# Two experts' rows per token added up in memory by the indirect transfers, instead of on VectorE in the last stage

## The chip, the cores and the metric

The kernel runs on one core of one Trainium2 chip. The metric is the device time of one execution in microseconds (us): 1415.3 us, the median of three runs of the kernel before (1413.99 to 1415.97).

## The reference

Two layers over x of 4 batches x 1024 tokens x 128 channels, float32. Each layer normalises x, computes an attention s and a gate g from it, and gives x + s * g. In the second layer, the gate is the silu of a mixture of experts:

```python
gates = softmax(xf @ Wg.T)                      # xf: T = 4096 tokens x 128
topw, topi = top_k(gates, 2)                    # two different experts for each token
C = round(2 * T * 1.05 / 8)                     # 1075 rows for each of the 8 experts
# each expert takes at most C (token, choice) entries, first choices first
h = gelu(rows @ W1[e] + b1[e]); y = h @ W2[e] + b2[e]
out[t] = sum over k of topw[t, k] * y[topi[t, k], position]     # 0 for an entry over the capacity
x = x + s * silu(out)
```

## The kernel before, in words

One program of seven stages, each a block in which every engine has its own list of instructions, ordered by semaphores. A stage begins when all engines have ended the one before. The two stages `inverse_and_routing` and `layer1_attention` also dispatch: for each of the two choices k, 32 indirect transfers (`dispatch`, L1259 to L1262) write 128 tokens' rows each into the memory table `x_disp`, at the row of the expert and position that the token was given. A row has 130 elements: the 128 channels, the number of the entry (k * 4096 + token, plus 1; 0 in a row that nobody fills) and its weight. `mark_entries` (L1252) sets the last two columns ahead of each k. `x_disp` and the result table `y_tok` are zeroed in pieces of about 1 MB by SyncE during the first layer's attention (`zero`, L804), one piece in each of the first `PIECES` = 18 turns of its loop (14 pieces for `x_disp`, 4 for `y_tok`).

`experts` (from L1701) treats the eight experts one after the other, as j = 0 to 3 and buffer c = 0 or 1. SyncE loads an expert's 1075 rows (9 tiles of 128, the last of 51) and weights. TensorE transposes the rows (L1843), multiplies by W1 (L1855), and, after the gelu on ScalarE (L1835), by W2 in three groups of tiles (L1865). VectorE copies the transposed rows (L1779), works out where each row's result goes (L1784 to L1789: `wt`, `free`, `dest`), adds the bias (L1800) and multiplies by the weight (L1807). Before L1784 VectorE waits until the transfers out of this buffer for the expert two earlier have landed (L1782). SyncE's load of the next rows into a buffer waits for `dest`. GpSimd then sends the rows by nine indirect transfers per expert (L1765), each as soon as its group has been multiplied. A row goes to row `k * 4096 + token` of `y_tok`, so no two experts write the same row; results of unfilled rows go to spare rows behind. The last expert has groups of 3, 3 and 3 tiles, and its matmuls are interleaved. GpSimd waits for all landings before the stage ends (L1768).

`combine` (from L1911) works in 8 parts of 4 token tiles (128 x 512 elements). SyncE issues two loads per part, one per choice (L1955, 16 in all, 256 KB each), VectorE adds the two (L1935), ScalarE takes the silu (L1946), VectorE multiplies by the attention (L1928) and adds to x (L1930), and SyncE stores the part (L1959). SyncE's stores stand behind all its loads. VectorE does the next part's sum before it finishes a part.

Of the kernel before, what the change touches and what calls it, by code (L numbers as in the profile page):

```python
# [12 lines left out]
P = 128  # L13
# [13 lines left out]
NPAIR = B * PAIRS  # L27
E, TOPK = 8, 2
CAP = int(round(TOPK * B * T * 1.05 / E))
ENTRIES = TOPK * B * T  # L30
XT = -(-CAP // P)
LASTROWS = CAP - (XT - 1) * P
HID = 512
# [35 lines left out]
def make(nc, ctx, ins):  # L69
    g = Program()  # L70
    g.nc = nc
    (g.x_in, g.ln_scale, g.ln_bias, g.w_qkv, g.w_proj, g.b_proj, g.W_r, g.W_k, g.W_v, g.mu_r, g.mu_k,
     g.W_attn, g.W_proj, g.Wg, g.W1, g.b1, g.W2, g.b2, g.out) = ins
    g.sb = lambda name, shape, dt=F32: ctx.enter_context(nc.sbuf_tensor(name, shape, dt))
    sems = {}

    def sem(name):
        if name not in sems:
            sems[name] = nc.alloc_semaphore(name=name)
        return sems[name]  # L80

    cleared = []

    def clear(eng, prefix):

        for name in [n for n in sems if n.startswith(prefix)]:
            eng.sem_clear(sems[name])
            cleared.append(sems.pop(name))

    def release():  # L90

        while cleared:
            nc.release_semaphore(cleared.pop())

    g.sem, g.clear, g.release = sem, clear, release
    g.dram = lambda name, shape, dt=F32: nc.dram_tensor(name, shape, dt, kind="Internal").ap()
    g.ps = ctx.enter_context(nc.psum_tensor("psum", [P, 8 * BANK], F32))
    g.bank = lambda k, n=1: g.ps[:, k * BANK:(k + n) * BANK]


    g.X = g.sb("x_res", [P, NT, D])
    g.XNW = g.sb("x_norm", [P, NT, ROW])
    g.XN = g.XNW[:, :, 0:D]
    g.G = g.sb("gate_or_attn", [P, NT, D])

    g.ident = g.sb("ident", [P, P])
    g.wqkv0 = g.sb("wqkv0", [P, 3, P])
    g.wproj0 = g.sb("wproj0", [P, P])
    g.wr2 = [g.sb(f"wr{i}", [P, P]) for i in range(2)]
    g.wk2 = [g.sb(f"wk{i}", [P, P]) for i in range(2)]  # L110
    g.wvT = g.sb("wvT", [P, P])
    g.wqkv1 = g.sb("wqkv1", [P, 3 * P])
    g.wproj1 = g.sb("wproj1", [P, P])
    g.wgT = g.sb("wgT", [P, E])
    g.b1T = g.sb("b1T", [P, E * HC])
    g.cols = g.sb("cols", [P, 8])
    g.bproj = g.sb("bproj", [P, P])
    g.eps_pow = g.sb("eps_pow", [P, TB])
    g.mask4 = g.sb("mask4", [P, 4])
    g.headmask = g.sb("headmask", [P, H])  # L120


    g.q_ops = g.dram("q_ops", [QUADS, HQ, NPART, HD, T], BF16)
    g.k_ops = g.dram("k_ops", [QUADS, HQ, 2 * NPART - 1, HD, T], BF16)
    g.v_ops = g.dram("v_ops", [QUADS, P, HQ, TB * 2 * HD])
    g.av_out = g.dram("av_out", [QUADS, HQ, 2 * HD, T])
    g.x_disp = g.dram("x_disp", [E * CAP + ENTRIES, ROW])
    g.y_tok = g.dram("y_tok", [ENTRIES + 2 * XT * P, D])
    g.recs = g.dram("recs", [B, H, T])
    g.q1_keep = g.dram("q1_keep", [B, P, T])  # L130
    return g
# [43 lines left out]
E_RING = 12  # L175
DISP_ROW = CAP * ROW // 5
DISP_PIECES = -(-DISP_ROW // 2048)
PIECES = DISP_PIECES + ENTRIES * D // P // 2048
LOADS0 = 16 * (4 * NPART + 1)
STORED = (48, 48, 32)  # L180

# [383 lines left out]
def layer0_attention(g):  # L565
# [31 lines left out]
    with nc.Block() as block:  # L597
# [183 lines left out]
        @block.sync  # L781
        def _(sp):
            def store_maxima(d):


                for i in range(NPART):
                    if i == 0:
                        sp.wait_ge(sem("b_max_done"), seq.index((d, None)) + 1)
                    else:
                        sp.wait_ge(sem(("b_second", "b_third")[i - 1]), d + 1)  # L790
                    dst = q[d // 2 % SLOTS][ROWS + i:ROWS + i + 1, 2 * (d % 2):2 * (d % 2) + 2, :]
                    sp.dma_start(dst.rearrange("r h (t x) -> r (h t) x", x=P), neg[:, i, :])\
                      .then_inc(sem("b_m_loaded"), 16)

            def store_values(d):
                sp.wait_ge(sem("b_acc"), d + 1)
                for i in range(4):
                    dst = g.av_out[d // 2, 2 * (d % 2) + i // 2, :, i % 2 * BANK:(i % 2 + 1) * BANK]
                    sp.dma_start(dst, acc[32 * i:32 * i + 2 * HD, d % 2, :]).then_inc(sem(f"b_stored{d % 2}"), 16)

            disp = g.x_disp[0:E * CAP, :].rearrange("(q r) d -> q (r d)", q=E * 5)
            kept = g.y_tok[0:ENTRIES, :].rearrange("(q r) d -> q (r d)", q=P)

            def zero(piece):  # L804
                i = 2048 * piece
                if piece < DISP_PIECES:
                    n = min(2048, DISP_ROW - i)
                    sp.dma_start(disp[:, i:i + n], zeros[0:E * 5, 0:n]).then_inc(sem("disp_zeroed"), 16)
                else:
                    i -= 2048 * DISP_PIECES  # L810
                    sp.dma_start(kept[:, i:i + 2048], zeros[:, :]).then_inc(sem("disp_zeroed"), 16)

            for c in range(1, SLOTS):
                load_quad(g, sp, c, c)
            store_maxima(0)
            sp.wait_ge(sem("b_zeros"), 1)
            for d in range(DUOS):
                if d + 1 < DUOS:
                    store_maxima(d + 1)
                store_values(d)  # L820
                if d < PIECES:
                    zero(d)
                if d % 2 and d // 2 + SLOTS < QUADS:

                    sp.wait_ge(sem("b_av"), TB * (d + 1))
                    wait_for_parts(g, sp, (d // 2 + SLOTS) // 4)
                    load_quad(g, sp, d // 2 + SLOTS, d // 2 % SLOTS)
            for s in range(2):
                sp.wait_ge(sem(f"b_stored{s}"), 16 * 4 * QUADS)
            sp.wait_ge(sem("disp_zeroed"), 16 * PIECES)  # L830

# [419 lines left out]

def mark_entries(g, link, k):  # L1252

    link(g.nc.gpsimd.tensor_scalar(g.XNW[:, :, D:D + 1], g.iof[:, E + k * NT:E + (k + 1) * NT].unsqueeze(2),
                                   float(1 - E * CAP), None, ALU.add))
    link(g.nc.gpsimd.tensor_copy(g.XNW[:, :, D + 1:D + 2], g.CW[:, k, :].unsqueeze(2)))


# [451 lines left out]
def experts(g):  # L1710
# [31 lines left out]
    with nc.Block() as block:  # L1742
# [11 lines left out]
        @block.gpsimd  # L1754
        def _(pool):
            nc.gpsimd.tensor_scalar(unused[:, :, :], g.iof[:, E:E + 2 * XT].rearrange("p (c t) -> p c t", c=2),
                                    float(ENTRIES + 1 - E * CAP), None, ALU.add).then_inc(sem("e_unused"), 1)
            for j in range(E // 2):
                for c in range(2):
                    pool.wait_ge(sem("e_dest"), ex(j, 1, c, 1))  # L1760
                    for i, (lo, hi) in enumerate(groups(j, c)):
                        pool.wait_ge(sem("e_y"), ex(j, 3, c, i + 1))
                        for t in range(lo, hi):
                            r = rows(t)
                            pool.indirect_dma_start(g.y_tok[:, :], bass.IndirectOffsetOnAxis(dest[c][0:r, t:t + 1], 0),  # L1765
                                                    y[c][0:r, t, :], None).then_inc(sem(f"e_sent{c}"), 16)
            for c in range(2):
                pool.wait_ge(sem(f"e_sent{c}"), SENT * (E // 2))  # L1768

# [141 lines left out]
def combine(g):  # L1911

    nc, sem = g.nc, g.sem
    with ExitStack() as mem:
        sb = lambda name, shape, dt=F32: mem.enter_context(nc.sbuf_tensor(name, shape, dt))
        yk = sb("g_y", [P, TOPK, NT, D])
        f = sb("g_f", [P, NT, D])
        sg = sb("g_sg", [P, NT, D])
        spare = sb("g_spare", [P, 1])
    part = lambda i: slice(i * NT // PARTS, (i + 1) * NT // PARTS)  # L1920
    with nc.Block() as block:

        @block.vector
        def _(dve):
# [5 lines left out]
                nc.vector.tensor_tensor(g.X[:, s, :], g.X[:, s, :], sg[:, s, :], ALU.add).then_inc(sem("g_x"), 1)  # L1930

            for i in range(PARTS):
                s = part(i)
                dve.wait_ge(sem(f"g_loaded{i}"), 16 * TOPK)
                nc.vector.tensor_tensor(f[:, s, :], yk[:, 0, s, :], yk[:, 1, s, :], ALU.add).then_inc(sem("g_f"), 1)  # L1935
                if i >= 1:
                    finish(i - 1)
            finish(PARTS - 1)

        @block.scalar  # L1940
        def _(act):
            act.activation(spare[:, :], g.eps_pow[:, 0:1], ACT.Silu).then_inc(sem("g_spare"), 1)
            for i in range(PARTS):
                s = part(i)
                act.wait_ge(sem("g_f"), i + 1)
                act.activation(sg[:, s, :], f[:, s, :], ACT.Silu).then_inc(sem("g_sg"), 1)  # L1946

        @block.sync
        def _(sp):
            src = g.y_tok[0:ENTRIES, :].rearrange("(k n p) d -> p k n d", p=P, k=TOPK)  # L1950
            dst = g.out.rearrange("b (n p) d -> p (b n) d", p=P)
            for i in range(PARTS):
                s = part(i)
                for k in range(TOPK):
                    sp.dma_start(yk[:, k, s, :], src[:, k, s, :]).then_inc(sem(f"g_loaded{i}"), 16)  # L1955
            for i in range(PARTS):
                s = part(i)
                sp.wait_ge(sem("g_x"), i + 1)
# [43 lines left out]
```

## Time and profile before

| | |
|---|---|
| Median of three runs | 1415.3 us |
| The profiled execution's own time | 1400.87 us |
| Its span in the trace | 1399.1 us |
| Busy in the span: PE, DVE, ACT, POOL | 90%, 72%, 62%, 17% |
| Expert stage, from its first matmul to the start of the last stage | 1225.7 to 1375.3 us |
| Last stage | 1375.3 to 1399.1 us |

Times in the trace are counted from the start of its span. PE is TensorE, PEld its weight loads, DVE VectorE, ACT ScalarE, POOL GpSimd, SPq SyncE's queue of transfer issues. A POOL DMA_INDIRECT row shows the time that GpSimd needs to issue the transfer, and not the movement of the data. "Idle before" is the time in which an engine had nothing running ahead of an instruction, with the instruction that ended it.

### The profile page before, as it was taken

To read this page: it belongs to the slowest core of one execution; us is meant where nothing else is said; L and a number is where in the kernel's file an instruction comes from. 1 tells how busy PE (TensorE), PEld (TensorE's weight loads), DVE (VectorE), ACT (ScalarE), POOL (GpSimd) and SP (SyncE) were. 2 spreads that over 40 slices of the span, in tenths; PEclk is the share of its full clock that TensorE was granted. 3 is DMA by queue.
4 is the path that set the end of the run, shared out by engine and by line. 5 is a ranking of instruction groups with operands and counts; after the bars stand their busy time and mean duration, and the time that the engine had idled before them with its cause. 6 is when DMAs were issued, how large, how long until landed. Compare 5 with 4: busy or idle time off the path is not lost. (4 is left out here: it accounts for less than half of the span.)

```text
span 1399.1 us, 26250 instructions
## 1 busy us (share of the span) xinstructions
PE 1265.2 (90%) x10433; PEld 595.5 (43%) x10433; DVE 1009.8 (72%) x1309; ACT 864.0 (62%) x1459; POOL 236.2 (17%) x306
## 2 busy tenths in 40 slices
PE   6967999999999999999999988898899899999990
PEld 4631222222222222222222235555699666678870
DVE  6877888898998988899899637665756388623324
ACT  3533878788887787888888855555132466543331
POOL 4200110000000000000000011100644222125560
PEclk9976999999999999999999989999999699999995
DMA  4763133331334323322120021100001111123316
GB/s 145 214 189 67 32 67 84 71 71 47 67 86 98 108 78 72 67 62 48 27 64 10 6 55 33 46 16 15 18 28 34 59 35 43 47 65 99 100 57 186
DMA packets 75206, 94.98 MB, mean 68 GB/s; under 512 B 13236, under 2 KB 44684, under 8 KB 74052
## 3 DMA queue, kind: packets, MB, share of 16 engines
q1 hardware_dynamic: 69996, 83.19, 23.6%
q0 software_dynamic: 5088, 10.12, 2.3%
q8 instruction: 82, 1.34, 0.4%
q14 instruction: 40, 0.33, 0.1%
HBM read 54.30 MB, written 38.56 MB: 66 GB/s over the span
## 5 line engine op out<-in xcount | busy, mean ns | idle before, releaser
L664 ACT ACTIVATE b_exp_ring<-psum 128x512 f32<-128x512 f32 x1024 | 555.5, 599 | 158.2 <-PE psum L719 155.0
L606 DVE TENSOR_REDUCE b_mx<-psum 128x2 f32<-128x1024 f32 x507 | 595.8, 1219 | 75.9 <-PE psum L551 74.8
L719 PE MATMUL psum<-b_q,b_k 75*128 75x512 bf16 x1024 | 311.9, 387 | 10.7 <-DMA b_q<-b_neg 9.1
L695 PE MATMUL psum<-b_exp_ring,b_v 128*32 128x512 f32 x2048 | 274.5, 608 | 0.9 <-ACT b_exp_ring L664 0.7
L719 PEld LDWEIGHTS psum<-b_q,b_k 75*128 75x128 bf16 x1024 | 79.2, 97 | 328.4 <-ACT b_exp_ring L664 223.6
L550 PE MATMUL psum<-b_k,b_q 64*128 64x512 bf16 x512 | 169.0, 395 | 25.4 <-DVE b_mx L606 10.5
L551 PE MATMUL psum<-b_ko,b_qo 64*128 64x512 bf16 x512 | 169.0, 395 | 0.0
L734 POOL CAST b_neg<-b_neg_rest 16x128 bf16<-16x128 f32 x32 | 8.9, 280 | 661.4 <-DVE b_neg_rest L617 661.4
L1835 ACT ACTIVATE e_hT<-psum,e_b 128x358 f32<-128x358 f32 (+3 forms) x96 | 53.7, 560 | 75.6 <-PE psum L1855 72.3
L550 PEld LDWEIGHTS psum<-b_k,b_q 64*128 64x128 bf16 x512 | 44.1, 93 | 127.5 <-DVE b_mx L606 41.8
L695 PEld LDWEIGHTS psum<-b_exp_ring,b_v 128*32 128x32 f32 x2048 | 41.2, 108 | 108.2 <-issue 106.4
L1261 POOL DMA_INDIRECT x_disp<-x_norm,row_sent x64 | 62.5, 976 | 122.1 <-PE psum L1633 81.4
L1765 POOL DMA_INDIRECT y_tok<-e_y,e_dest x72 | 70.8, 984 | 70.7 <-DVE e_y L1807 51.5
L1865 PE MATMUL psum<-e_w,e_hT 128*128 128x128 f32 (+1 forms) x576 | 67.4, 277 | 0.0
L1569 DVE TENSOR_REDUCE f_max<-psum 128x16 f32<-128x1024 f32 x32 | 39.2, 1225 | 37.3 <-PE psum L1633 36.5
L1865 PEld LDWEIGHTS psum<-e_w,e_hT 128*128 128x128 f32 (+1 forms) x576 | 64.6, 184 | 1.8
L1613 ACT ACTIVATE f_le<-f_lx 128x1024 f32<-128x1024 f32 x32 | 33.8, 1057 | 47.3 <-DVE f_lx L1575 47.3
L1855 PE MATMUL psum<-e_xT,e_w 128*128 128x358 f32 (+3 forms) x192 | 60.2, 468 | 0.9 <-DVE e_xT L1779 0.9
L991 DVE TENSOR_REDUCE c_nm<-psum 128x1 f32<-128x1024 f32 x32 | 37.7, 1220 | 31.7 <-PE psum L1148 31.6
L1411 ACT ACTIVATE i_aq<-psum 128x1024 f32<-128x1024 f32 x20 | 20.5, 1024 | 58.7 <-PE psum L1434 58.7
L1095 ACT ACTIVATE c_en<-psum,c_nm 128x1024 f32<-128x1024 f32 x32 | 35.7, 1117 | 32.1 <-DVE c_nm L991 32.1
L1434 PE MATMUL psum<-i_x,i_aq 64*64 64x64 f32 x1536 | 46.2, 218 | 1.4 <-DVE i_x L1380 1.4
(281 smaller groups left out, 1487.4 us busy)
## 6 DMA issues: line engine op xcount, KB each, us to landing
b_q<-q_ops SPq DMA_DIRECT2D x48, 192.0 KB
b_k<-k_ops SPq DMA_DIRECT2D x48, 192.0 KB
k_ops<-a_k SPq DMA_DIRECT2D x20, 256.0 KB, 3.2
x_disp<-b_zeros SPq DMA_DIRECT2D x13, 320.0 KB
e_x<-x_disp SPq DMA_DIRECT2D x8, 520.0 KB
v_ops<-a_vs SPq DMA_DIRECT2D x4, 1024.0 KB, 5.1
b_v<-v_ops SPq DMA_DIRECT2D x16, 256.0 KB
av_out<-b_acc SPq DMA_DIRECT2D x128, 32.0 KB, 1.7
```

Of the source, the lines that this page charges most:

```text
L550: g.nc.tensor.matmul(g.bank(2 * (n % 2)), q[0:MROWS, 2 * p, t], k[0:MROWS, 2 * p, keys], start=True, stop=True)
L551: return g.nc.tensor.matmul(g.bank(2 * (n % 2) + 1), qo[MROWS:P, p, t], ko[MROWS:P, p, keys], start=True, stop=True)
L606: nc.vector.reduce_max(mx[:, d % 2, :, i // 2, i % 2], pair, AX.X).then_inc(sem("b_max_done"), 1)
L664: act.activation(ex[:, n % E_RING, :], g.bank(5 + n % 3), ACT.Exp, scale=ATT_SCALE)\
L695: last = nc.tensor.matmul(AV[32 * i:32 * i + 32, :], v[s][:, at_v:at_v + 32], ex[:, (4 * group + i) % E_RING, :], start=(kb == 0), stop=(k ...
L719: nc.tensor.matmul(g.bank(5 + n % 3), k[s][0:XROWS, h, kb * P:(kb + 1) * P], q[s][0:XROWS, h, half * BANK:(half + 1) * BANK], start=True, ...
L1261: pool.indirect_dma_start(g.x_disp[:, :], bass.IndirectOffsetOnAxis(g.rows_out[:, n:n + 1], 0), g.XNW[:, n % NT, :], None).then_inc(g.sem( ...
L1434: last = nc.tensor.matmul(out[half, i, :], lhs(n * GR + i, half), rhs(n * GR + i, half), start=True, stop=True)
L1765: pool.indirect_dma_start(g.y_tok[:, :], bass.IndirectOffsetOnAxis(dest[c][0:r, t:t + 1], 0), y[c][0:r, t, :], None).then_inc(sem(f"e_sent ...
L1835: act.activation(hT[c][:, i, lo:hi], g.ps[:, (3 + n % 3) * BANK:(3 + n % 3) * BANK + hi - lo], ACT.Gelu, bias=b1[c][:, i:i + 1]).then_inc( ...
L1855: nc.tensor.matmul(g.ps[:, (3 + n % 3) * BANK:(3 + n % 3) * BANK + hi - lo], w1[c][:, i * P:(i + 1) * P], xT[:, lo:hi], start=True, stop=T ...
L1865: last = nc.tensor.matmul(g.ps[0:r, col:col + D], hT[c][:, i, t * P:t * P + r], w2[c][:, i, :], start=(i == 0), stop=(i == HC - 1))
```

## The change

`y_tok` with a row per entry becomes `y_sum` with a row per token. The number in a dispatched row is that of the token, whichever choice it is, so `mark_entries` writes that column for k = 0 only. The indirect transfers of the experts add their rows to the table (`compute_op=ALU.add`). As a token's two experts now write the same row, GpSimd waits, ahead of each expert's transfers, until those of the expert before have landed. Only 2 pieces of the table are zeroed, where 4 were. The last stage loads one row per token, takes its silu and does the two operations that are left on VectorE.

```diff
-PIECES = DISP_PIECES + ENTRIES * D // P // 2048
+PIECES = DISP_PIECES + TOKENS * D // P // 2048
...
-    link(g.nc.gpsimd.tensor_scalar(g.XNW[:, :, D:D + 1], g.iof[:, E + k * NT:E + (k + 1) * NT].unsqueeze(2),
-                                   float(1 - E * CAP), None, ALU.add))
+    if k == 0:
+        link(g.nc.gpsimd.tensor_scalar(g.XNW[:, :, D:D + 1], g.iof[:, E:E + NT].unsqueeze(2),
+                                       float(1 - E * CAP), None, ALU.add))
...
                 for c in range(2):
                     pool.wait_ge(sem("e_dest"), ex(j, 1, c, 1))
+                    if c or j:
+                        pool.wait_ge(sem(f"e_sent{1 - c}"), SENT * (j + c))
                     for i, (lo, hi) in enumerate(groups(j, c)):
                         pool.wait_ge(sem("e_y"), ex(j, 3, c, i + 1))
                         for t in range(lo, hi):
                             r = rows(t)
-                            pool.indirect_dma_start(g.y_tok[:, :], bass.IndirectOffsetOnAxis(dest[c][0:r, t:t + 1], 0),
-                                                    y[c][0:r, t, :], None).then_inc(sem(f"e_sent{c}"), 16)
+                            pool.indirect_dma_start(g.y_sum[:, :], bass.IndirectOffsetOnAxis(dest[c][0:r, t:t + 1], 0),
+                                                    y[c][0:r, t, :], None, compute_op=ALU.add).then_inc(sem(f"e_sent{c}"), 16)
...
             for i in range(PARTS):
-                s = part(i)
-                dve.wait_ge(sem(f"g_loaded{i}"), 16 * TOPK)
-                nc.vector.tensor_tensor(f[:, s, :], yk[:, 0, s, :], yk[:, 1, s, :], ALU.add).then_inc(sem("g_f"), 1)
-                if i >= 1:
-                    finish(i - 1)
-            finish(PARTS - 1)
+                finish(i)
...
-                act.wait_ge(sem("g_f"), i + 1)
-                act.activation(sg[:, s, :], f[:, s, :], ACT.Silu).then_inc(sem("g_sg"), 1)
+                act.wait_ge(sem(f"g_loaded{i}"), 16)
+                act.activation(sg[:, s, :], yk[:, s, :], ACT.Silu).then_inc(sem("g_sg"), 1)
...
-                for k in range(TOPK):
-                    sp.dma_start(yk[:, k, s, :], src[:, k, s, :]).then_inc(sem(f"g_loaded{i}"), 16)
+                sp.dma_start(yk[:, s, :], src[:, s, :]).then_inc(sem(f"g_loaded{i}"), 16)
```

## Rows read from the trace of the kernel before

**Rows 1.** Windows: us, busy (count) of PE, PEld, DVE, ACT, POOL; clock, DMA share, GB/s.

```profile
1242.49:1259.33 16.84, 16.84 (x108) 13.58 (x107) 5.14 (x13) 6.71 (x12) 8.92 (x10) 1.00 0.24 68
...
1343.54:1375.30 31.76, 17.85 (x116) 14.51 (x114) 5.32 (x12) 6.72 (x12) 17.69 (x18) 0.81 0.12 35
1375.30:1399.10 23.80, 0.00 (x0) 0.00 (x0) 15.34 (x24) 6.52 (x10) 0.00 (x0) 0.50 0.98 265
```

**Rows 2.** Timeline of the last stage (start, us, operation [idle before]), then the chain's start.

```profile
1379.56 0.69 DVE L1935 TENSOR_TENSOR g_f<-g_y 128x512 f32<-128x512 f32 x1 [16.87 <-DMA g_y<-y_tok]
1380.29 0.63 ACT L1946 ACTIVATE g_sg<-g_f 128x512 f32<-128x512 f32 x1 [3.40 <-DVE g_f L1935]
...
1382.11 0.69 DVE L1928 TENSOR_TENSOR g_sg<-g_sg,gate_or_attn 128x512 f32<-128x512 f32 x1
...
1382.83 0.69 DVE L1930 TENSOR_TENSOR x_res<-x_res,g_sg 128x512 f32<-128x512 f32 x1
1383.44 0.69 DVE L1935 TENSOR_TENSOR g_f<-g_y 128x512 f32<-128x512 f32 x1
...
1395.74 0.69 DVE L1930 TENSOR_TENSOR x_res<-x_res,g_sg 128x512 f32<-128x512 f32 x1
...
1375.38 0.38 SPq L1955
...
1375.81 0.50 SPq L1955
```

**Rows 3.** DMA view of the last stage, 1375 to 1399.1 us, in 40 slices.

```profile
GB/s 0 0 54 249 332 275 185 252 320 334 293 298 292 296 292 291 287 292 291 289 292 290 287 293 290 289 292 321 349 343 348 343 347 345 235 303 133 246 190 0
```

**Rows 4.** Timeline around the third expert's first transfer; the other boundaries look the same.

```profile
1259.32 1.00 POOL L1765 DMA_INDIRECT y_tok<-e_y,e_dest  x1 [5.48 <-DVE e_y L1807]
...
1269.53 1.08 POOL L1765 DMA_INDIRECT y_tok<-e_y,e_dest  x1 [0.30 <-issue]
...
1272.25 0.17 DVE L1784 COPY e_wt<-e_x 128x9 f32<-128x9 f32 x1 [1.35 <-DMA y_tok<-e_y,e_dest]
...
1274.34 0.69 DVE L1800 TENSOR_TENSOR e_y<-psum,e_b 128x512 f32<-128x512 f32 x1 [1.64 <-PE psum L1865]
1275.06 0.69 DVE L1807 TENSOR_TENSOR e_y<-e_y,e_wt 128x512 f32<-128x512 f32 x1
1276.51 0.99 POOL L1765 DMA_INDIRECT y_tok<-e_y,e_dest  x1 [5.90 <-DVE e_y L1807]
```

**Rows 5.** Timeline of the last two experts' transfers up to the last stage.

```profile
1353.77 1.07 POOL L1765 DMA_INDIRECT y_tok<-e_y,e_dest  x1 [0.30 <-issue]
...
1355.89 0.99 POOL L1765 DMA_INDIRECT y_tok<-e_y,e_dest  x1 [1.05 <-DVE e_y L1807]
...
1366.42 1.07 POOL L1765 DMA_INDIRECT y_tok<-e_y,e_dest  x1 [0.30 <-issue]
```

**Rows 6.** DMA view of 1366.3 to 1375 us, in 40 slices of 0.22 us.

```profile
DMA  0450000032000000000000000000000000000000
```

**Rows 7.** GpSimd's queue in the DMA view of 1240 to 1400 us: packets, MB, share of 16 engines.

```profile
q0 software_dynamic: 2560, 4.41, 8.7%
```

**Rows 8.** Tile views of the two tables that indirect transfers write: count, ns min/median/max.

```profile
L1765 POOL DMA_INDIRECT y_tok<-e_y,e_dest x72: 963/967/1089, 1242.5 to 1366.4; - x72
...
L1261 POOL DMA_INDIRECT x_disp<-x_norm,row_sent x64: 954/957/1410, 1020.3 to 1210.7; - x64
```

**Rows 9.** Waits in 1240 to 1400 us: total, times, longest.

```profile
DVE e_wt L1784 <- DMA y_tok<-e_y,e_dest: 9.7, 6, 2.6
```

**Rows 10.** Timeline: GpSimd ahead of the second choice's dispatch, and a zeroing issue.

```profile
1098.85 0.33 POOL L1254 TENSOR_SCALAR x_norm<-r_iota 128x32 f32<-128x32 f32 x1
...
1100.87 1.06 POOL L1261 DMA_INDIRECT x_disp<-x_norm,row_sent  x1 [1.39 <-PE psum L1633]
...
500.40 0.42 SPq L811 DMA_DIRECT2D y_tok<-b_zeros  x1
```

**Rows 11.** SyncE's own waits, whole span: the zeroing stands in this loop.

```profile
SPq L799 <- ACT b_acc L656: 239.9, 32, 16.6
```

More of the change, by code:

```diff
@@ L29 @@
 CAP = int(round(TOPK * B * T * 1.05 / E))
-ENTRIES = TOPK * B * T
+TOKENS = B * T
+ENTRIES = TOPK * TOKENS
 XT = -(-CAP // P)
@@ L127, in make @@
     g.x_disp = g.dram("x_disp", [E * CAP + ENTRIES, ROW])
-    g.y_tok = g.dram("y_tok", [ENTRIES + 2 * XT * P, D])
+    g.y_sum = g.dram("y_sum", [TOKENS + 2 * XT * P, D])
     g.recs = g.dram("recs", [B, H, T])
@@ L801, in _ @@
             disp = g.x_disp[0:E * CAP, :].rearrange("(q r) d -> q (r d)", q=E * 5)
-            kept = g.y_tok[0:ENTRIES, :].rearrange("(q r) d -> q (r d)", q=P)
+            kept = g.y_sum[0:TOKENS, :].rearrange("(q r) d -> q (r d)", q=P)
             def zero(piece):
@@ L1756, in _ @@
             nc.gpsimd.tensor_scalar(unused[:, :, :], g.iof[:, E:E + 2 * XT].rearrange("p (c t) -> p c t", c=2),
-                                    float(ENTRIES + 1 - E * CAP), None, ALU.add).then_inc(sem("e_unused"), 1)
+                                    float(TOKENS + 1 - E * CAP), None, ALU.add).then_inc(sem("e_unused"), 1)
             for j in range(E // 2):
@@ L1915, in combine @@
         sb = lambda name, shape, dt=F32: mem.enter_context(nc.sbuf_tensor(name, shape, dt))
-        yk = sb("g_y", [P, TOPK, NT, D])
-        f = sb("g_f", [P, NT, D])
+        yk = sb("g_y", [P, NT, D])
         sg = sb("g_sg", [P, NT, D])
@@ L1944, in _ @@
                 s = part(i)
-                act.wait_ge(sem("g_f"), i + 1)
-                act.activation(sg[:, s, :], f[:, s, :], ACT.Silu).then_inc(sem("g_sg"), 1)
+                act.wait_ge(sem(f"g_loaded{i}"), 16)
+                act.activation(sg[:, s, :], yk[:, s, :], ACT.Silu).then_inc(sem("g_sg"), 1)
         @block.sync
         def _(sp):
-            src = g.y_tok[0:ENTRIES, :].rearrange("(k n p) d -> p k n d", p=P, k=TOPK)
+            src = g.y_sum[0:TOKENS, :].rearrange("(n p) d -> p n d", p=P)
             dst = g.out.rearrange("b (n p) d -> p (b n) d", p=P)
```

## The prediction

> **What bounds the kernel now.** I read the windows first, one per expert: in each of the six full periods, of which one is shown, TensorE is busy for all of 16.84 us, and GpSimd for 8.9 [rows 1]. Up to the seventh expert TensorE sets the pace. After it the picture turns: in the 31.76 us from the seventh expert's first transfer to the last stage TensorE is busy for 17.85 us, and GpSimd issues 18 transfers nearly back to back. The timeline shows the order there: the last issue ends at 1366.42 + 1.07 = 1367.49 us [rows 5], its data move until about 1368.7 us (slices 8 to 10) [rows 6], and the last stage begins at 1375.38 [rows 2]. So the end of the expert stage hangs on GpSimd's chain. What fills the 6.7 us between the data and the last stage no row shows; the change doesn't touch it, and I keep it.
>
> In the last stage VectorE is busy for 15.34 us with its 24 operations, 1.92 us for the three of a part [rows 1], and the timeline has it without a gap from its second sum on; the last operation ends at 1396.43 [rows 2]. The DMA engines are 98% busy there too: 265 GB/s for 23.8 us are 6.3 MB [rows 1]. Both would have to shrink for a gain, and the change shrinks both.
>
> **The last stage.** Removed per part: one load of 256 KB and L1935. What is left on VectorE is L1928 and L1930. From L1928 to L1930 is 0.72 us (1382.11 to 1382.83), from L1930 to the next operation 0.61 (1382.83 to 1383.44): 1.33 us per part [rows 2]. ScalarE's 0.63 us per part is below that. The start: now the first sum begins at 1379.56, when the part's second load has landed. One load is to come instead, whose issue starts 0.43 us before that of the second (1375.38 and 1375.81) [rows 2]: I take 1379.1 us. Then the silu, 0.63, and about 0.05 to the next engine: first multiplication at 1379.8. Seven parts of 1.33 and a last one of 0.72 + 0.69 end at 1390.5, against 1396.43. That is **5.9 us less**. The DMA engines allow it: 4.2 MB instead of 6.3 at the 290 GB/s of the middle slices [rows 3] are 14.5 us, from about 1376.6 to 1391.1, and the last store (2.7 us behind the last operation now) ends at 1393.2 by VectorE's account. If they became the limit, with reads and stores hindering each other at the 185 to 250 GB/s of the poorest slices, the gain would shrink to about 4.
>
> **The new wait, at today's prices.** GpSimd's cycle for an expert is nine issues, 1259.32 to 1269.53 + 1.08 = 1270.61, and the landing, which VectorE sees at 1272.25, 1.64 us later [rows 4]. With 0.4 us for GpSimd to wake (about half of the 0.76 us from the end of L1807, 1275.75, to the issue at 1276.51) that makes C = 13.3 us. The period is 16.84, so 3.5 us of C stay hidden for the first seven experts. VectorE waits for the same landing two experts later in a buffer's life; it has 1.64 us idle behind it [rows 4], and could be late by some 2 more, since TensorE needs its bank only for the third group, some 3 us after the first is done. What stands behind GpSimd's new wait is nothing but its own transfers. SyncE's loads wait for `dest` on VectorE, and are needed 12 us later.
>
> For the last expert there is no cover. Its first transfer starts at 1355.89, but the seventh's last issue ends at 1353.77 + 1.07 = 1354.84, plus 1.64 and 0.4 is 1356.9. From there nine issues at a pitch of 1.27 us (0.97 and 0.30 between two), as in the cycle above, end 11.3 us later, at 1368.2, instead of 1367.49; the small waits for groups among them are swallowed [rows 5]. **0.7 us more.**
>
> **The price of adding.** No row shows an accumulating transfer. Two unknowns: d, more time per issue, and L, more time to land. Call G = 9d + L the growth of C. In the tail it counts twice (seventh and eighth expert). Until C reaches 16.84, that is G = 3.5, it counts nowhere else.
> For d: from below 0, as more work can't be quicker to issue. From above, one more issue's time, 0.97 us. The nearest rows: rows of 512 and of 520 bytes take 0.967 and 0.957 us [rows 8], and the last of each expert, with 51 rows instead of 128, takes 1.07 to 1.09. The issue doesn't grow with the rows or bytes it is for, so I take d = 0.
> For L: from below 0, as it moves more. From above, a second landing in front of the first, 1.64 us; a landing that other traffic had slowed made VectorE wait 2.6 us where it usually waits 1.35 [rows 4, 9], so 1.3 more on top. The engines themselves have room: GpSimd's queue used 8.7% of 16 engines in 160 us, which over 72 transfers is 0.19 us per transfer and engine [rows 7], against a pitch of 1.27; even three times that keeps up. The 51 rows of an expert's last transfer, 0.6 us of movement [rows 6], may need as much again. I take the middle, L = 0.8. So G = 0.8, and the tail pays **1.6 us**.
>
> By the Trainium skill (Collectives: The Full Stack, "Why ReduceScatter is half of AllGather") a reducing transfer has two read descriptors where a copy has one, and half the rate. The rule alone would double the 0.19 us and leave my sum as it is; its bearing on the issue is the second rival.
>
> **Covered edits.** The 0.33 us of L1254 for k = 1 go, but GpSimd waits 1.39 us for TensorE ahead of its first transfer [rows 10], so nothing. The last two zeroing pieces (issues of 0.42 us, as at 500.40) [rows 10] go from a loop in which SyncE waits 239.9 us for ScalarE alone [rows 11], so nothing; 0 to 0.3 us if one of them had delayed a load.
>
> **Sum.** -5.9 + 0.7 + 1.6 = -3.6 us. It is made against the profiled execution (1400.87 us, its span 1399.1), which lies 14.4 us below the median of 1415.3; the stages concerned have no reason to differ, so 1415.3 - 3.6 = 1411.7 us. About 0.2%, 2.8 us, is what a measurement of this kernel can tell from no change: the forecast is just beyond.
>
> **The rivals.** In all of them the total is 0.7 + 2G - 5.9 while G < 3.5.
> *Given back in the tail (same).* G between 1.2 and 3.6: from -2.8 to +2.8 us. Say d = 0.1 and L = 1.2: G = 2.1, total -1.0, 1414.3 us. For it: the new wait exposes whatever latency the addition has, twice, and a single tenth of a microsecond per issue costs 1.8 us. Against: the flat issue times.
> *GpSimd becomes the bound (slower).* Beyond G = 3.5 the chain of waits and issues is longer than 16.84 us, and GpSimd's chain runs through all eight experts, from 1242.49 us to the end: 8 us for each us of G beyond. At G = 3.5 the total is +1.8; at 3.6 it passes +2.8. The place is L1765 behind the new wait; the price, with d = 0.4 and L = 0.8, is G = 4.4, so 1.8 + 8 x 0.9 = +9.0 us, 1424.3 us. With d = 0.97 it would be near 50 us. For it: an added row has two sources, the expert's result and the table's row; should the issue time follow their number, d is somewhere up to 0.97. Against: rows of 128 and 51 cost alike now. TensorE would then show idle time at L1865 and L1843 before a late VectorE.
> The Trainium skill (GPSIMD Engine Reference, section 4) has one GpSimd core emit the read descriptors and another the write descriptors; with the rule above, the reading core would have twice the work, which would put this rival at its upper end; no row here shows it.
> *The last stage gives less.* Loads and stores at the poorest rate: gain 4, total -1.7 us, 1413.6 us. It falls under "same".
> *The addition is nearly free.* G near 0: 0.7 - 5.9 = -5.2 us, 1410.1 us.
>
> **How the numbers follow.** The forecast, G about 0.8: 0.33. The addition nearly free: 0.10. Together, G below 1.2 and a full gain in the last stage, 0.43 faster. Given back in the tail, 0.24, and a poorer last stage, 0.07: 0.31 same. GpSimd as the bound, 0.26: slower. The range: from G = 0 with 0.8 us for the runs' own spread, 1409.3, to 1424, G = 4.4 in the slower case. That leaves some 4% below and 16% above. Faster and same alone span 1409.3 to 1418.1.
>
> **What would show each step.** The median of L1765 (0.967 us now) gives d. From the end of an expert's ninth issue to VectorE's L1784 gives 1.64 + L. Right, if TensorE still fills its 16.84 us per expert, if the last expert's first issue is near 1357.7, the last near 1368 to 1369 and the last stage starts near 1377.7; and if its L1930s are 1.33 us apart and the last ends 15.1 us after the first load's issue (1375.38 to 1390.5 on the old clock). Wrong, if GpSimd's idle time is put down to its own transfers' landing in all experts, if the periods grow beyond 16.84, or if parts of the last stage come at the loads' pace.

## The result: 2.2% slower

The changed kernel takes 1446.5 us (median of four runs, 1442.4 to 1447.6) against 1415.6 for the kernel before: a ratio of 1.022, interval 1.0197 to 1.0242, some 31 us more. Measured once more later, beside runs of the kernel before on one chip, the ratio was 1.0205 (1.0166 to 1.0245). Forecast were 1411.7 us and a range up to 1424.

**The profile after.** First the windows, as in [rows 1]: two of the stretches from an expert's first transfer to the next, then the seventh expert's to the last stage, then the last stage.

```profile
1273.08:1295.35 22.27, 18.60 (x104) 14.68 (x103) 5.37 (x14) 6.71 (x12) 14.63 (x10) 0.88 0.53 91
1295.35:1317.12 21.77, 18.36 (x110) 14.36 (x109) 5.31 (x14) 6.70 (x12) 14.66 (x10) 0.96 0.42 66
...
1383.19:1426.80 43.61, 16.86 (x97) 13.19 (x96) 4.50 (x11) 6.72 (x13) 28.90 (x18) 0.70 0.29 25
1426.80:1444.30 17.50, 0.00 (x0) 0.00 (x0) 10.44 (x16) 6.52 (x10) 0.00 (x0) 0.50 0.85 240
```

The last stage gained what was expected of it, 23.8 to 17.5 us. But a period is now 22 us, where it was 16.84. TensorE is idle for 1.8 to 5.1 us of it, and the granted clock is 0.88 to 0.97 in five of the six periods, where it was 1.00 in all six before. The tail grew from 31.8 to 43.6 us. Next, the tile view of the table and the waits (total, times, longest) from 1240 us on:

```profile
L1769 POOL DMA_INDIRECT y_sum<-e_y,e_dest x72: 1546/1556/2005, 1251.8 to 1418.2; - x72
```

```profile
DVE e_wt L1788 <- DMA y_sum<-e_y,e_dest: 52.0, 6, 10.5
POOL y_sum L1769 <- DVE e_y L1811: 47.8, 8, 18.2
...
PE psum L1869 <- DVE e_y L1804: 20.0, 6, 5.1
```

Two readings stand here. An adding transfer takes 1.556 us to issue, against 0.967 [rows 8]. And six times VectorE waits ahead of L1788 (L1784 of before) for a landing, 52.0 us in all where it was 9.7 [rows 9]. GpSimd's idle time is still put down to VectorE, as before, and hardly at all to the new wait. Only in the tail does it show, as 3.03 us of "issue" (a wait behind which the profile names no instruction):

```profile
1403.34 1.57 POOL L1769 DMA_INDIRECT y_sum<-e_y,e_dest  x1 [3.03 <-issue]
```

The timeline around the third expert's first transfer, to be held against [rows 4]:

```profile
1288.36 1.78 POOL L1769 DMA_INDIRECT y_sum<-e_y,e_dest  x1 [0.30 <-issue]
1292.42 0.17 DVE L1788 COPY e_wt<-e_x 128x9 f32<-128x9 f32 x1 [8.71 <-DMA y_sum<-e_y,e_dest]
...
1293.16 0.69 DVE L1804 TENSOR_TENSOR e_y<-psum,e_b 128x512 f32<-128x512 f32 x1 [0.29 <-issue]
...
1293.89 0.69 DVE L1811 TENSOR_TENSOR e_y<-e_y,e_wt 128x512 f32<-128x512 f32 x1
1293.91 1.53 PEld L1869 LDWEIGHTS psum<-e_w,e_hT 128*51 128x51 f32 x8 [3.86 <-DVE e_y L1804]
...
1295.35 2.00 POOL L1769 DMA_INDIRECT y_sum<-e_y,e_dest  x1 [5.20 <-DVE e_y L1811]
```

The last issue ends at 1290.14, the landing shows at 1292.42 (2.28 us, where it was 1.64; over the six experts 1.99 to 2.44), and then VectorE does the row numbers of the fourth expert, which has the same buffer, and only after them, late, the third's outputs, for which GpSimd waits. The landing comes back to GpSimd through VectorE, 2.9 us later. In the last stage, L1933 follows L1933 at the forecast 1.33 us:

```profile
1430.20 0.63 ACT L1944 ACTIVATE g_sg<-g_y 128x512 f32<-128x512 f32 x1 [1.90 <-DMA g_y<-y_sum]
...
1439.55 0.69 DVE L1933 TENSOR_TENSOR x_res<-x_res,g_sg 128x512 f32<-128x512 f32 x1
...
1440.88 0.69 DVE L1933 TENSOR_TENSOR x_res<-x_res,g_sg 128x512 f32<-128x512 f32 x1
```

### The profile page after: what moved, and what is told of

Its sections match the earlier page's. It is cut to its first block and busy times, and to the rows that moved or that the text cites. A ratio compares the mean times of both kernels' runs of the same rounds, so it can differ in the third digit from the quotient of the medians.

```text
span 1444.3 us, 26231 instructions
## 1 busy us (share of the span) xinstructions
PE 1281.4 (89%) x10433; PEld 605.5 (42%) x10433; DVE 1004.1 (70%) x1301; ACT 863.8 (60%) x1459; POOL 281.4 (19%) x305
## 5 line engine op out<-in xcount | busy, mean ns | idle before, releaser
L551 PE MATMUL psum<-b_k,b_q 64*128 64x512 bf16 x512 | 168.5, 394 | 25.7 <-DVE b_mx L607 10.6
L1769 POOL DMA_INDIRECT y_sum<-e_y,e_dest x72 | 116.4, 1617 | 70.0 <-DVE e_y L1811 47.8
L1869 PE MATMUL psum<-e_w,e_hT 128*128 128x128 f32 (+1 forms) x576 | 70.6, 283 | 20.0 <-DVE e_y L1804 20.0
L1869 PEld LDWEIGHTS psum<-e_w,e_hT 128*128 128x128 f32 (+1 forms) x576 | 66.6, 187 | 22.3 <-DVE e_y L1804 21.1
L1859 PE MATMUL psum<-e_xT,e_w 128*128 128x358 f32 (+3 forms) x192 | 68.1, 514 | 0.9 <-DVE e_xT L1783 0.9
L992 DVE TENSOR_REDUCE c_nm<-psum 128x1 f32<-128x1024 f32 x32 | 37.7, 1219 | 31.8 <-PE psum L1149 31.8
L1413 ACT ACTIVATE i_aq<-psum 128x1024 f32<-128x1024 f32 x20 | 20.5, 1023 | 63.5 <-PE psum L1436 63.5
L1436 PE MATMUL psum<-i_x,i_aq 64*64 64x64 f32 x1536 | 50.5, 219 | 3.1 <-DVE i_x L1382 1.5
```

What stands on the lines that cost most here:

```text
L551: g.nc.tensor.matmul(g.bank(2 * (n % 2)), q[0:MROWS, 2 * p, t], k[0:MROWS, 2 * p, keys], start=True, stop=True)
L1436: last = nc.tensor.matmul(out[half, i, :], lhs(n * GR + i, half), rhs(n * GR + i, half), start=True, stop=True)
L1769: pool.indirect_dma_start(g.y_sum[:, :], bass.IndirectOffsetOnAxis(dest[c][0:r, t:t + 1], 0), y[c][0:r, t, :], None, compute_op=ALU.add).t ...
L1859: nc.tensor.matmul(g.ps[:, (3 + n % 3) * BANK:(3 + n % 3) * BANK + hi - lo], w1[c][:, i * P:(i + 1) * P], xT[:, lo:hi], start=True, stop=T ...
L1869: last = nc.tensor.matmul(g.ps[0:r, col:col + D], hT[c][:, i, t * P:t * P + r], w2[c][:, i, :], start=(i == 0), stop=(i == HC - 1))
```

## The experiments

The theories: **A**, the price of an adding issue, in a chain that VectorE's older wait (L1782 of before) closes for every expert: landing, VectorE, outputs of the next expert, GpSimd. **B**, the new wait on GpSimd is what costs.

The whole time of one execution is a blunt measure here. The start of the first transfer, ahead of which no experiment changes anything but the two zeroing pieces and one small operation, lay between 1239.2 and 1258.9 us in the twelve profiled executions. The kernel before itself took 1402.8 to 1415.6 us beside the different runs, so times are compared by their ratio to it. Beside each ratio the table has two stretches from the trace: S, from the first transfer of an expert to the start of the last stage, and the last stage. S is no exact measure either: e6 and e8 leave all of it as it was and have 135.3 us, 2.4 more than before.

| | ratio to before (interval) | S, us | last stage, us |
|---|---|---|---|
| before | 1 | 132.9 | 23.7 |
| changed | 1.022 (1.0197 to 1.0242) | 175.0 | 17.5 |
| e1 adding only | 1.0291 (1.0252 to 1.0331) | 172.4 | 24.1 |
| e2 new wait only | 1.0005 (0.9985 to 1.0026) | 133.9 | 24.2 |
| e3 changed, plain transfers | 0.9942 (0.9922 to 0.9963) | 134.0 | 17.4 |
| e4 changed, older wait moved | 1.0153 (1.0113 to 1.0193) | 164.2 | 17.4 |
| e5 changed again | 1.0205 (1.0166 to 1.0245) | 174.5 | 17.4 |
| e6 last stage only | 0.9946 (0.9924 to 0.9968) | 135.3 | 17.3 |
| e8 sum on GpSimd | 1.0027 (1.0001 to 1.0052) | 135.3 | 26.5 |
| e10 adding only, older wait moved | 1.0054 (1.0034 to 1.0074) | 143.7 | 23.8 |

**e1, adding only.**

```diff
-                                                    y[c][0:r, t, :], None).then_inc(sem(f"e_sent{c}"), 16)
+                                                    y[c][0:r, t, :], None, compute_op=ALU.add).then_inc(sem(f"e_sent{c}"), 16)
```

> The kernel before, with only the adding put into the expert transfers (table of a row per entry as before, no new wait, last stage as before). Theory A, the issue price and the old wait: an adding issue takes 1.55 us instead of 0.97, and VectorE's older wait for a landing (ahead of the row numbers, in front of the next expert's outputs) already ties each expert's first transfer to the landing of the one before, so the periods become 22 us without any new wait, and only the last expert is freed of it (some 3 us): about 1450 us, 34 above before. Theory B, the new wait is what costs: TensorE keeps nearly its 16.84 us per expert, at most 17.4 (nine issues of 1.85), and the time is 5 to 15 us above before, 1421 to 1430.

Theory A's case. The runs are 2.9% slower, 39 us between the medians, where A expected 34 and B 5 to 15. S is 172.4 us, 2.6 short of the changed kernel's, without any new wait, and VectorE's wait is to a tenth the same:

```profile
DVE e_wt L1784 <- DMA y_tok<-e_y,e_dest: 52.0, 6, 10.5
POOL y_tok L1765 <- DVE e_y L1807: 46.1, 8, 16.5
```

The periods are those of the changed kernel too (21.4, 22.3, 21.8, 22.0, 22.2, 22.0). Only at the last expert does GpSimd go straight on, 0.31 us after the seventh's last issue, where the changed kernel had 3.03:

```profile
1386.58 1.76 POOL L1765 DMA_INDIRECT y_tok<-e_y,e_dest  x1 [0.30 <-DVE e_y L1807]
1388.65 1.57 POOL L1765 DMA_INDIRECT y_tok<-e_y,e_dest  x1 [0.31 <-issue]
```

**e2, the new wait only.**

```diff
                     pool.wait_ge(sem("e_dest"), ex(j, 1, c, 1))
+                    if c or j:
+                        pool.wait_ge(sem(f"e_sent{1 - c}"), SENT * (j + c))
```

> The kernel before, with only GpSimd's new wait, plain transfers. Theory A: hidden for seven experts, exposed once in the tail: 0.7 to 1.3 us more, 1416.3 to 1417. Theory B, the new wait is what costs: 10 us more or above.

With plain transfers the wait is worth 1.0 us of S, which by itself is within what S varies, and nothing that the runs can tell. The steps from one first issue to the next are those of before to within 0.03 us up to the seventh expert. The wait shows at one place, the last expert:

```profile
1356.14 1.07 POOL L1767 DMA_INDIRECT y_tok<-e_y,e_dest  x1 [0.30 <-issue]
1359.53 0.99 POOL L1767 DMA_INDIRECT y_tok<-e_y,e_dest  x1 [2.32 <-DMA y_tok<-e_y,e_dest]
```

From the end of the issue, 1357.21, it takes 2.32 us: the landing's 1.64 and 0.7 for GpSimd to go on. Whether it is felt there depends on TensorE. In e6, without the new wait, TensorE's results come later, and the same transfer starts 3.52 us behind the issue before it; the wait would have been covered:

```profile
1363.35 1.08 POOL L1765 DMA_INDIRECT y_tok<-e_y,e_dest  x1 [0.30 <-issue]
1367.95 0.99 POOL L1765 DMA_INDIRECT y_tok<-e_y,e_dest  x1 [3.53 <-DVE e_y L1807]
```

**e3, everything but the adding.**

```diff
-                                                    y[c][0:r, t, :], None, compute_op=ALU.add).then_inc(sem(f"e_sent{c}"), 16)
+                                                    y[c][0:r, t, :], None).then_inc(sem(f"e_sent{c}"), 16)
```

> The changed kernel with plain transfers in place of adding ones: a token keeps the row of whichever expert wrote last, so the sum of two experts is left out. Theory A: periods back at 16.84 us, the last stage keeps its gain of 6.3, the wait in the tail costs 1: about 5 us below before, 1410 to 1411. Theory B: still 15 us or more above before.

A row of the table holds what the last of its two experts wrote, without the sum. The whole loss is gone with the one argument: 0.58% faster than before, 7 to 8 us where 5 were expected, S back at 134.0, the last stage at 17.4. B is out with e1 to e3. It also shows what the change was worth, had the adding been free.

**e4, the older wait moved.** The row numbers get a second table per buffer, so that only the outputs need the earlier transfers to have landed.

```diff
-        dest = [sb(f"e_dest{c}", [P, XT], I32) for c in range(2)]
+        dest = [[sb(f"e_dest{c}{i}", [P, XT], I32) for i in range(2)] for c in range(2)]
...
                 if before:
-                    dve.wait_ge(sem(f"e_sent{c}"), j * SENT)
+                    dve.wait_ge(sem("e_y"), ex(j - 1, 3, c, 3))
...
             def outputs(j, c):
                 dve.wait_ge(sem(f"e_w_loaded{c}"), j * WLOADS + WLOADS)
                 dve.wait_ge(sem("e_wt"), ex(j, 1, c, 1))
+                if j:
+                    dve.wait_ge(sem(f"e_sent{c}"), j * SENT)
```

> The changed kernel with VectorE's older wait for a landing moved from ahead of the row numbers to ahead of the same expert's outputs, a whole expert later, with two tables of row numbers per buffer. Theory A: the return from a landing to the next first issue no longer leads through VectorE (2.9 us) but directly (0.75): a period of nine issues 17.1 + landing 2.3 + 0.75 = 20.1 us instead of 22.1, over six or seven experts 12 to 15 us less than the changed kernel, 1432 to 1435. If the issue price alone sets the period, no gain: 1446.

S falls by 10.8 us, a little short of the 12 to 15 expected, and the ratio from 1.022 to 1.0153. GpSimd now waits for the landing alone (the "issue" of 2.97 us):

```profile
1358.19 1.77 POOL L1769 DMA_INDIRECT y_sum<-e_y,e_dest  x1 [0.31 <-issue]
1362.94 1.56 POOL L1769 DMA_INDIRECT y_sum<-e_y,e_dest  x1 [2.97 <-issue]
```

Six of the seven steps from one first issue to the next are 19.6 to 20.1 us, as worked out. The one from 1280.89 on is 22.39, 2.6 more than the others' mean: the gap behind its last issue is 5.73 us instead of 2.9 to 3.1. SyncE had issued the loads of the next weights and rows just ahead:

```profile
1295.34 0.33 SPq L1504 DMA_DIRECT2D e_w<-in_L_ffn_W_dram  x1
1295.72 0.43 SPq L1505 DMA_DIRECT2D e_w<-in_L_ffn_W_dram  x1
1295.79 1.76 POOL L1769 DMA_INDIRECT y_sum<-e_y,e_dest  x1 [0.30 <-issue]
...
1296.74 0.44 SPq L1496 DMA_DIRECT2D e_x<-x_disp  x1
1297.22 1.06 SPq L1498 DMA_DIRECT2D e_x<-x_disp  x1
...
1303.28 1.57 POOL L1769 DMA_INDIRECT y_sum<-e_y,e_dest  x1 [5.73 <-issue]
```

That these loads hold the landing up is read from the order and was not tried by itself.

**e5, the changed kernel again**, unedited.

> The changed kernel once more, beside the kernel before on the same chip, since its profiled execution lost 8 us in the inverse stage, whose instructions it shares with the kernel before, and that of before was 14 us below its runs. If that loss belongs to the change, the inverse stage takes 120 us again; if it was that execution's own, 112 as in all other profiles. Ratio to before: 1.022 by the first measurement; from the experiments' parts, 1.029 less 3 us of tail and 6 of the last stage against adding alone... that is, adding alone +40 us, less 6, plus 3: +37 us, 1.026.

The ratio repeats (1.0205), and so does S (174.5). The inverse stage, from its first operation to that of the next stage, took 118.5 us, after 120.2 in the first profile of the changed kernel. But it took 111.3 to 112.5 in e1 to e4, adding or not, and 118.1 to 120.3 in e6 to e10, plain transfers or not. So its length goes with the occasion of the measurement and not with the change, and the expectation's alternatives didn't meet it.

**e6, the last stage only.** The kernel before with the last stage of the changed one, on the first choice's rows; the second's are left out.

```diff
-            src = g.y_tok[0:ENTRIES, :].rearrange("(k n p) d -> p k n d", p=P, k=TOPK)
+            src = g.y_tok[0:B * T, :].rearrange("(n p) d -> p n d", p=P)
```

> The kernel before with the changed last stage alone: it loads the first choice's rows only and leaves the second's out of the sum. Both theories: the last stage from 23.8 to 17.5 us, 6.3 us less, ratio 0.9955; the expert stage as before.

6.4 us less in the last stage and 0.54% (7.6 us, 0.32% to 0.76%) in the runs, as expected. The expert stage, which was expected as before, has an S of 135.3 us instead of 132.9; the 2.4 us are lost ahead of the last expert's first transfer (the rows under e2), and e8, which doesn't touch that stage either, loses them too. Why isn't known.

**e7 and e9, half the rows.** In the changed kernel and in that before, for every second expert 64 rows of a full tile are sent and the other 64 left out.

```diff
-                            r = rows(t)
+                            r = 64 if c == 0 and t < XT - 1 else rows(t)
```

> The changed kernel with only the first 64 rows of each full tile sent for every second expert (c = 0); the other rows are left out. If the issue of an adding transfer pays per row (0.59 us for 128 rows more than a plain one), an issue of 64 rows takes 1.26 us; if the addition adds a fixed piece, it stays at 1.55. If the landing's 0.64 us are the read of the table's rows, it changes little.

> The kernel before (plain transfers) with only the first 64 rows of each full tile sent for every second expert (c = 0); the other rows are left out. The adding transfer took 1.40 us to issue for 64 rows and 1.556 for 128, 2.4 ns per row. If the addition costs a fixed piece and the rows cost alike with and without it, a plain issue of 64 rows takes 0.81 us; if the rows' price is the addition's (read descriptors of the table), it stays at 0.96.

The issues, adding (e7), at 64 rows (first line) and at 128 (second):

```profile
1254.58 1.39 POOL L1769 DMA_INDIRECT y_sum<-e_y,e_dest  x1 [0.30 <-issue]
...
1273.72 1.56 POOL L1769 DMA_INDIRECT y_sum<-e_y,e_dest  x1 [0.30 <-issue]
```

and plain (e9):

```profile
1263.84 0.90 POOL L1765 DMA_INDIRECT y_tok<-e_y,e_dest  x1 [0.30 <-issue]
...
1282.21 0.97 POOL L1765 DMA_INDIRECT y_tok<-e_y,e_dest  x1 [0.30 <-issue]
```

Neither reading was right alone. Between 64 and 128 rows a plain row costs about 1.0 ns ((0.97 - 0.907) / 64), an added one 2.4 ((1.556 - 1.40) / 64). Of the 0.59 us, 0.18 are then the rows' and 0.41 don't depend on them. The price doesn't carry on to fewer rows: the last transfer of an expert, with 51, takes longer than a full one, 1.07 to 1.09 us plain and 1.76 to 1.78 adding, and no run tells why. So fewer, fuller transfers would be the way to make adding cheap, and these are full already. The landing behind e7's halved experts, 1.94 to 2.36 us, is as with full ones, but the transfer that lands last there, with its 51 rows, was not changed. Both kernels leave results out and ran once each. S is 169.4 us in e7, and 141.7 in e9, more than the 132.9 of before with less to send; that isn't explained, and only the issue times are used here.

The Trainium skill (GPSIMD Engine Reference, section 4) gives the read descriptors to one GpSimd core and the write descriptors to another. The Trainium skill (Collectives: The Full Stack, "Why ReduceScatter is half of AllGather") gives two reads to each reduced piece. The rows' part, 2.4 ns against 1.0, grows in that sense, which doesn't prove it, and is the smaller part of the 0.59 us.

**e8, the sum on GpSimd.** The kernel before, with L1935 moved to GpSimd.

```diff
+        @block.gpsimd
+        def _(pool):
+            for i in range(PARTS):
+                s = part(i)
+                pool.wait_ge(sem(f"g_loaded{i}"), 16 * TOPK)
+                nc.gpsimd.tensor_tensor(f[:, s, :], yk[:, 0, s, :], yk[:, 1, s, :], ALU.add).then_inc(sem("g_f"), 1)
```

> The kernel before with the sum of the two rows (L1935) moved to GpSimd, which is idle in the last stage. If VectorE's three operations set the last stage's pace, 2 to 5 us less (ratio 0.997 to 0.9985), ending where the DMA engines' 6.3 MB end, some 22 us after the stage begins; if the DMA engines set it, or a sum takes GpSimd 2 us or more, no change or slower.

An attempt to have part of the gain without adding in memory. It failed: 2 to 5 us less were hoped for, and the runs are 0.27% slower (0.01% to 0.52%). The last stage takes 26.5 us, 2.8 more, and not because GpSimd is too slow, at 1.26 to 1.80 us per sum: VectorE is never idle once it has begun. VectorE's own operations suffer beside it:

```profile
1396.67 1.26 POOL L1940 TENSOR_TENSOR g_f<-g_y 128x512 f32<-128x512 f32 x1 [0.42 <-DMA g_y<-y_tok]
1396.94 1.54 DVE L1928 TENSOR_TENSOR g_sg<-g_sg,gate_or_attn 128x512 f32<-128x512 f32 x1 [18.74 <-ACT g_sg L1948]
...
1398.51 0.69 DVE L1930 TENSOR_TENSOR x_res<-x_res,g_sg 128x512 f32<-128x512 f32 x1
```

The seven of VectorE's sixteen operations that begin while a sum runs take 1.54 to 1.75 us, the other nine 0.68 or 0.69; the one at 1398.51 begins 0.06 us ahead of a sum. Each of the seven ends 0.54 or 0.55 us behind the end of the sum that it ran into (the first at 1398.48, its sum at 1397.93): read from these times, it is held up until the sum ends, and not slowed throughout. The Trainium skill says that GpSimd shares its SBUF interfaces with VectorE, and names operations with two SBUF inputs (GPSIMD Engine Reference, section 8). This trace agrees: L1928 and L1930 have two.

**e10, adding only, older wait moved.** The edits of e1 and e4 together, on the kernel before, no new wait.

> The kernel before with the adding and with VectorE's older wait moved a whole expert later, no new wait on GpSimd, last stage as before. Nothing ties a first issue to the landing before it any more: only the issue price is left, a period of 9 x 1.85 + 0.2 = 16.9 us or little more, just above TensorE's 16.84, and a tail of 18 issues each 0.59 us dearer, 10.6 us: about 12 to 14 us above before, ratio 1.009 to 1.010. If landings still hold it (their engines busy with three times the work), 20 us or more.

The price of the issues alone: S is 10.8 us longer, and the runs are 0.54% (7.6 us, 0.34% to 0.74%). The 12 to 14 expected were a little high. The row before each expert's first issue shows GpSimd without a pause; the fifth expert starts 16.98 us after the fourth:

```profile
1308.61 1.76 POOL L1765 DMA_INDIRECT y_tok<-e_y,e_dest  x1 [0.30 <-DVE e_y L1809]
1310.68 1.57 POOL L1765 DMA_INDIRECT y_tok<-e_y,e_dest  x1 [0.31 <-issue]
...
1325.58 1.78 POOL L1765 DMA_INDIRECT y_tok<-e_y,e_dest  x1 [0.30 <-DVE e_y L1809]
1327.66 1.57 POOL L1765 DMA_INDIRECT y_tok<-e_y,e_dest  x1 [0.30 <-issue]
```

So the landings don't hold GpSimd once no wait asks for them.

The six full periods add only 1.8 us together. The other 9.0 come from the last two experts, whose 18 issues cost 0.59 us more each, 10.6 us in all, less what they cover of the pauses that were there before. With e1, e10 and the changed kernel, the loss in the trace splits into parts: the issues +10.8 us (e10 against before), the older wait's chain +28.7 (e1 against e10), the new wait +2.6 (changed against e1), the last stage -6.2. Together the parts are +35.9, against some 31 between the medians. The 5 us between the two stay unexplained; the stages ahead of the experts vary by more than that from one profiled execution to another.

The shares of the two waits depend on the order in which they are put in. Where no wait ties an expert's first transfer to the landing before it, S is 143.7 us (e10); with the new wait alone it is 164.2 (e4), with the older one alone 172.4 (e1), with both 175.0. So what costs is that an expert waits for the landing of the one before, whichever wait asks for it: 20.5 us on the straight way, and 28.7 through VectorE.

No run that adds beats the kernel before. Even the barest adding costs more in the trace (10.8) than the last stage gives back (6.2); by the runs the two are alike, 0.54% each (e10 and e6), and they were not run together. With the shared rows e10's way would also leave the landings of two experts unordered, which no run here tried.

## Why the prediction was wrong

**The last stage: right.** Forecast were 1.33 us per part, a last operation 15.1 us after the first load's issue, and 5.9 us of gain. Measured are 1.33, 14.8 (1426.79 to 1441.57) and 6.2, and e6 has the gain by itself.

**The new wait at plain prices: right.** 0.7 us forecast, 1.0 in e2, hidden for seven experts. That the numbers are so near is in part luck, since S varies by 2.4. The step for GpSimd to go on was 0.7 us instead of 0.4.

**d = 0: the step that failed.** The text reasoned that the issue doesn't grow with the rows or bytes it is for, and took no price for the addition. That an issue is flat in the size of a plain transfer says little of another kind of transfer, which has a fixed piece of its own: 0.41 us, and 1.4 ns per row more. d was 0.59 us, and nine of them are 5.3 us per expert. The bound of 0.97 held it; the choice within the bounds did not. L, taken as 0.8, was 0.64, near the upper end of the 0.35 to 0.80 us that the six landings have above 1.64.

**The cycle without VectorE: the second error.** I counted 3.5 us of slack, on a cycle of issues, landing and GpSimd's wake. But VectorE's list has the wait for expert (j, 0)'s landing, with the row numbers behind it, ahead of the outputs of expert (j, 1), for which GpSimd waits: the same landing, on the same cycle, not "two experts later in a buffer's life". The return costs 2.9 us and not 0.4, and the first issue beside VectorE's late operations takes 2.0 us and not 1.56. With d = 0.59 and L = 0.64, G is 5.95 and the text's own sum gives 1.8 + 8 x 2.45 = 21 us more. The chain through VectorE makes the rest: 22.0 us per period instead of the 19.3 of that sum. e4, which takes VectorE out, has 19.8 (without its one long step). That the older wait was already an ordering of neighbours also makes the new one nearly redundant, which the text missed.

**The rival that came true** is "GpSimd becomes the bound", with its place and one of its signs, TensorE's idle time at L1869 (L1865 of before) ahead of a late VectorE, 20.0 us in six places. It was given 0.26, and priced at d = 0.4 without the chain. Two other signs came otherwise than named: TensorE has no such idle time at L1847 (L1843 of before), and GpSimd's is put down to VectorE and not to its own landings, because the chain leads through VectorE. By the text's formula the total passes +2.8 us at G = 3.63 and not 3.6, which changes nothing. A price that counts nine times per expert, and that no row shows, should have been given more weight above zero.

**The covered edits** cost nothing that a run could tell. They lie ahead of S, so the ratios have to tell: 0.9942 for e3, which has them all beside the new wait, and 0.9946 for e6, which has none. Each is known to 0.2%, some 3 us.

## What to carry to other kernels

Price a transfer of a new kind by a run of its own before trusting it on a queue that is half full: here nine issues took 11.3 of a period's 16.84 us, 0.59 us more on each filled it, and the work saved elsewhere (6 us, once) was below what the last two experts' 18 issues cost more in e10 (9 us). Before adding a wait, look for one that already orders the same two things on another engine's list; the path from a landing to the next issue takes in whatever stands behind the wait on that list (a gap of 4.6 to 5.2 us here, and 2.9 to 3.1 straight). Moving such a wait to where its data are really needed took one more table per buffer and was worth some 11 us of S here.

## What was not expected of the hardware

An adding indirect transfer of 128 rows of 512 bytes took 1.556 us to issue, a plain one 0.967. On the DMA engines it took more than double the time as well. GpSimd's queue in the view of the changed kernel from 1240 to 1450 us has

```profile
q0 software_dynamic: 11520, 4.42, 23.6%
```

for the same 4.4 MB as in [rows 7]. That is 4.5 times the packets, and 0.236 x 210 / 72 = 0.69 us per transfer and engine instead of 0.19, 3.6 times. An estimate by the half rate that the Trainium skill has for reducing transfers (Collectives: The Full Stack, "Why ReduceScatter is half of AllGather") would be 0.38 us; the measured one is nearly twice that. It still fits into a pitch of 1.86 us, and e10 shows that it sets no pace.
